# Two thirds and half of the scan steps fed row-wise instead of three fifths and seven fifteenths, in a Mamba, attention and expert block on one Trainium2 core

## The reference, cut to what matters

```
x (8, 256, 256), ctx (8, 256, 256); 2 Mamba layers, d_inner 512, d_state 64
for each layer:                                # x = x + mamba(mamba(x)), then layernorm
    u, z = split(x @ in_w.T);  u = silu(causal_conv4(u))
    dt, B, C = split(u @ xp_w.T);  dt = softplus(dt @ dtw.T + dtb)
    for t in 256:  h = h * exp(dt_t * A) + (dt_t * u_t) * B_t        # h: 512 x 64
                   y_t = (h * C_t).sum(state)
    out = ((y + u * D) * silu(z)) @ out_w.T
x = layernorm(x + attention(q from x, k and v from ctx))
x = layernorm(x + top-2-of-8 experts(x), hidden 1024)
```

## Time and profile before

| | |
|---|---|
| median of 3 runs | 3373.1 us (3371.58 to 3378.8) |
| the profiled execution's own time | 3370.43 us |
| its span | 3368.7 us |
| VectorE busy | 3042.1 us, 90% of the span |
| ScalarE busy | 2746.9 us, 82% |
| TensorE matmuls | 2734.9 us, 81% |
| GpSimd busy | 2671.6 us, 79% |
| granted TensorE clock, mean | 0.946 |

### The profile page before, as it was taken

The page is one execution under the profiler, slowest core; times in us unless marked ns, Lnnn a source line. Parts: engine busy times, 40 slices in busy tenths (PEclk is TensorE's granted clock), DMA queues, the critical chain, the costliest instruction groups (busy, mean ns, idle before and its releaser), DMA issues.

```text
span 3368.7 us, 54626 instructions
## 1 busy us (share of the span) xinstructions
PE 2734.9 (81%) x19466; PEld 2403.0 (71%) x19466; DVE 3042.1 (90%) x2196; ACT 2746.9 (82%) x6432; POOL 2671.6 (79%) x1299
## 2 busy tenths in 40 slices
PE   5878788888778877888888888878888777888876
PEld 4767677777767766777776777767777666777665
DVE  4999999999999999999999999999999999999500
ACT  6979898898978897897989888898898869888422
POOL 5989998898989788787888888787887878877401
PEclk7999999999999999999999999999999979999988
DMA  2242111111111113223231333313222122433485
GB/s 94 90 140 70 45 51 49 51 55 45 49 58 53 39 51 104 95 82 114 95 119 64 110 117 120 126 67 127 100 102 93 49 82 86 146 124 128 133 283 186
DMA packets 151747, 319.34 MB, mean 95 GB/s; under 512 B 28570, under 2 KB 44963, under 8 KB 151092
## 3 DMA queue, kind: packets, MB, share of 16 engines
q1 hardware_dynamic: 147522, 305.08, 27.1%
q0 software_dynamic: 3072, 8.39, 0.7%
q10 hardware_dynamic: 882, 2.38, 0.2%
HBM read 285.90 MB, written 29.88 MB: 94 GB/s over the span
## 4 chain that ended last, share of the span: by engine, by line
DVE 27%; issue 26%; ACT 17%; PE 15%; POOL 14%; DMA 1%; SPq 0%; POOLq 0%; DVEq 0%; ACTq 0%
DVE h L1128 14%; POOL hC L904 12%; DVE psX L1118 9%; ACT dA L1096 8%; PE psY L1395 4%; PE psG L1342 4%; ACT xs L1067 3%; PE psX L1379 2%; PE psX L1377 1%; PE psG L1421 1%; PE psX L1342 1%; PE psX L1421 1%; ACT gT L953 1%; ACT diag_b L1065 1%; DVE gT L1142 1%
## 5 line engine op out<-in xcount | busy, mean ns | idle before, releaser
L904 POOL TENSOR_TENSOR hC<-h,cb 128x1024 f32<-128x1024 f32 x1024 | 2406.0, 2371 | 464.2 <-DVE h L1128 457.2
L1128 DVE TENSOR_TENSOR_SCAN h<-dA,psX 128x1024 f32<-128x1024 f32 (+1 forms) x1115 | 2305.6, 2101 | 69.7 <-PE psX L1379 33.8
L1096 ACT ACTIVATE dA<-dt,negA 128x255 f32<-128x255 f32 x4096 | 1716.6, 503 | 103.2 <-DVE h L1128 99.9
L1395 PE MATMUL psY<-ident,hC 128*128 128x128 f32 x8192 | 1121.4, 282 | 48.6 <-DVE gT L1142 38.4
L1395 PEld LDWEIGHTS psY<-ident,hC 128*128 128x128 f32 x8192 | 976.0, 146 | 62.6 <-DVE gT L1142 42.0
L1118 DVE TENSOR_TENSOR psX<-dtu,psX 128x1024 f32<-128x1024 f32 x513 | 619.3, 1207 | 47.1 <-POOL dtu L846 35.5
L1379 PE MATMUL psX<-ident,xs 128*128 128x128 f32 x3280 | 462.0, 287 | 158.8 <-ACT xs L1067 79.6
L1067 ACT ACTIVATE xs<-dtuT,bT 128x512 f32<-128x512 f32 x820 | 546.0, 719 | 13.6 <-PE psX L1379 13.0
L1379 PEld LDWEIGHTS psX<-ident,xs 128*128 128x128 f32 x3280 | 383.9, 147 | 235.2 <-ACT xs L1067 150.1
L1366 PE MATMUL psX<-ident,bT 128*128 128x128 f32 x1026 | 218.6, 296 | 193.4 <-DVE h L1128 191.0
L1366 PEld LDWEIGHTS psX<-ident,bT 128*128 128x128 f32 x1026 | 118.3, 142 | 299.2 <-DVE h L1128 279.3
(11 more groups left out here) (198 smaller groups left out, 2000.8 us busy)
## 6 DMA issues: line engine op xcount, KB each, us to landing
cb<-c_dram SPq DMA_DIRECT2D x256, 512.0 KB, 3.7
w_up<-in_w_exp SPq DMA_DIRECT2D x196, 256.0 KB, 3.0
w_down<-in_w_exp SPq DMA_DIRECT2D x196, 256.0 KB, 3.0
dA<-in_w_exp SPq DMA_DIRECT2D x44, 256.0 KB, 4.3
h<-in_w_exp SPq DMA_DIRECT2D x44, 256.0 KB, 4.8
x_slots<-got SPq DMA_DIRECT2D x16, 512.0 KB, 5.4
xg<-x_slots SPq DMA_DIRECT2D x60, 128.0 KB, 2.8
y_slots<-yg SPq DMA_DIRECT2D x60, 128.0 KB, 3.1
```

The costliest lines, as they stand in the source:

```text
L904: eng.tensor_tensor(hC[i % NHC][:, :, :], h[i % NH][:, :, :], cw.to_broadcast([P, KI, L]), ALU.mult).then_inc(times_c, 1)
L1096: made = eng.activation(dA[j % NA][:, c, 1:L], dt[n % 2][:, c, 1:L], ACT.Exp, scale=negA[:, JOBS[n][0], c, s:s + 1])
L1128: made = eng.tensor_tensor_scan(h[i % NH][:, part, :].rearrange("p c t -> p (c t)"), dA[i % NA][:, part, :].rearrange("p c t -> p (c t)"), ...
L1395: made = eng.matmul(psY[:, tc, c * P:(c + 1) * P], hC[i % NHC][:, c, tc * P:(tc + 1) * P], ident[:, :], start=s == 0 and c == 0, stop=s == ...
```

## The change

Of the steps of jobs 0 to 5, 20 in 30 are row-wise instead of 18; of those of jobs 6 to 13, 15 in 30 instead of 14; jobs 14 and 15 stay at 14. In jobs 0 to 5 every row-wise step that follows a plain one is of form D (before, a third of them was X). `xs` becomes two tiles used in turn (NX), so that `scale_row` waits for the X step before the last. The press on rank 0 starts at s = 30 with 150 ns a step instead of at s = 44 with 300. `xrow` of the next row is loaded at the piece `norm2` of this row instead of at the next row's `turn`, and the plan places `proj` of a row only after `norm2` of the row before. The counts that follow from `is_turned` and `is_scaled_later`:

| | row-wise | D | X | plain |
|---|---|---|---|---|
| jobs 0 to 5, before | 221 | 101 | 120 | 163 |
| jobs 0 to 5, after | 244 | 122 | 122 | 140 |
| jobs 6 to 13, before | 232 | 0 | 232 | 280 |
| jobs 6 to 13, after | 256 | 0 | 256 | 256 |
| jobs 14 and 15, both | 58 | 0 | 58 | 70 |

After the change the steps run `. D X` over and over in jobs 0 to 5, and `. X` in jobs 6 to 13.

```diff
-SHARE = [18] * 6 + [14] * (NJ - 6)
+SHARE = [20] * 6 + [15] * (NJ - 8) + [14] * 2
...
-    return 12 < i < STEPS and (s + 1) * SHARE[job] // 30 > s * SHARE[job] // 30
+    return 12 < i < STEPS and s >= 0 and (s + 1) * SHARE[job] // 30 > s * SHARE[job] // 30
...
-    return is_turned(i) and not is_turned(i - 1) and i < 6 * S and i % 3 != 0
+    return is_turned(i) and not is_turned(i - 1) and i < 6 * S
...
-LIKE_IT = {i: max((t for t in TURNED if t < i and is_scaled_later(t) == is_scaled_later(i)), default=None) for i in TURNED}
+LIKE_IT = {i: [t for t in TURNED if t < i and is_scaled_later(t) == is_scaled_later(i)] for i in TURNED}
+TILES_OF = {False: NX, True: 1}
+SAME_TILE = {i: before[-TILES_OF[is_scaled_later(i)]] if len(before) >= TILES_OF[is_scaled_later(i)] else None for i, before in LIKE_IT.items()}
...
-PRESS_FROM, PRESS = 44, 300
+PRESS_FROM, PRESS = 30, 150
...
-        out += [task("proj", b, 0, "PE", 2 * MM, *copied, opens="G"),
+        out += [task("proj", b, 0, "PE", 2 * MM, *copied, *((("norm2", b - 1, 0),) if b else ()), opens="G"),
...
-                    at["ACT"] = scaled[i] = max(at["ACT"], fill_end.get(LIKE_IT[i], never)) + (600 if is_scaled_later(i) else SCALE)
+                    at["ACT"] = scaled[i] = max(at["ACT"], fill_end.get(SAME_TILE[i], never)) + (600 if is_scaled_later(i) else SCALE)
...
-        xs = sb("xs", [P, KL, DI])
+        xs = [sb(f"xs{i}", [P, KL, DI]) for i in range(NX)]
...
-                        on.wait_ge(normed[1], b)
-                        eng.dma_start(xrow[:, :, :], io["x"][b]).then_inc(xrow_in, 16)
+                            eng.dma_start(xrow[:, :, :], io["x"][0]).then_inc(xrow_in, 16)
+                    elif name == "norm2" and n + 1 < ROWS:
+                        on.wait_ge(normed[1], n + 1)
+                        eng.dma_start(xrow[:, :, :], io["x"][n + 1]).then_inc(xrow_in, 16)
...
-                if LIKE_IT[i] is not None:
-                    on.wait_ge(x_in, LIKE_IT[i] + 1)
+                at = len(LIKE_IT[i]) % NX
+                if SAME_TILE[i] is not None:
+                    on.wait_ge(x_in, SAME_TILE[i] + 1)
```

More of the change, by code:

```diff
@@ L37 @@
 NW = 3
+NX = 2
 NT = 9
@@ L1066, in scale_row @@
                     else:
-                        made = eng.activation(xs[:, tc, :], dtuT[n % 2][:, tc, :], ACT.Identity, scale=bT[n % 2][:, tc, s:s + 1])
+                        made = eng.activation(xs[at][:, tc, :], dtuT[n % 2][:, tc, :], ACT.Identity, scale=bT[n % 2][:, tc, s:s + 1])
                 made.then_inc(scaled, 1)
@@ L1378, in turn_x @@
                         else:
-                            made = eng.transpose(to, xs[:, tc, c * P:(c + 1) * P], ident[:, :])
+                            made = eng.transpose(to, xs[len(LIKE_IT[i]) % NX][:, tc, c * P:(c + 1) * P], ident[:, :])
                 made.then_inc(x_in, 1)
```

## The result

| | before | after |
|---|---|---|
| median of 19 runs | 3376.1 us | 3384.9 us |
| ratio | | 1.0022, 95% interval 1.0012 to 1.0032 |
| profiled execution | 3370.4 us | 3388.5 us |
| granted TensorE clock, mean | 0.946 | 0.948 |

A forecast was written before the change was run, and what follows sets the result against it. The prediction took VectorE to set the loop's pace. Its terms, -59.2 + 8 + 5 + 12 - 2 = -36.2 us, gave a span of 3332.5 us and a forecast median of 3337 us, range 3312 to 3366.

The forecast's parts named there:

- The first term: In jobs 0 to 13, 47 plain steps become row-wise, each saving VectorE 1.26 us: 59.2 us less.
- More waits on VectorE: In the loop, X fills made late by ScalarE's in-order queue: +8 us in jobs 0 to 5, +5 in jobs 6 to 13.
- The order of the small work: After the loop, 3 to 4 more expert tiles left over by the plan, room for 2 during routing: +12 us.
- The third, that the tiles pile up: After the loop, 13 more tiles left, 11 of them bare: +88 us instead of +12, 3413 us; chance 0.10.
- The second: Jobs 0 to 5: ScalarE takes over as pacing engine, 17 us plus some 6 us more waits, 3360 us; chance 0.15.
- the case with a chance of 0.08: After the loop, a backlog of 5 to 8 tiles eats the gain to about nothing; chance 0.08.
- The first, the full gain: Whole kernel: no term beside the 59.2 us costs anything, giving 3314 us; chance 0.17.
- over 250 us after the loop: Sign that the forecast is wrong: the part after the loop, expected at about 230 us, lasts over 250.
- ScalarE in jobs 1 to 5: Sign that the forecast is wrong: ScalarE is busy over 95% in jobs 1 to 5.
- The second `xs` tile: On ScalarE, freeing its waits for a fill to release xs: worth 0 to 13 us, taken as 0.
- `xrow` at -2 us: After the loop, row 7's early load lets its first use start sooner: 0 to 5.2 us, taken as -2.
- Waits in jobs 6 to 13 at +5: VectorE's idle time in jobs 6 to 13 grows as ScalarE fills: bounds 0 and +15 us, taken as +5.

The follow-up runs named there:

- e4: e3 with 15 in 30 steps row-wise in jobs 6 to 13 and the plan's ScalarE costs at 1650 ns (dA) and 1300 ns (X); ratio 0.9887 to before.
- e5: e4 with the share of jobs 6 to 13 back at 14 in 30; ratio 0.9979 to the kernel before.
- e7: e1 with the silu replaced by a copy, so without both table loads a job (output not the reference's); ratio 0.9885 to the kernel before.
- e8: The kernel before with the silu replaced by a copy, without both table loads a job (output not the reference's); ratio 0.9940 to the kernel before.
- e1: The change in jobs 0 to 5 alone, with jobs 6 to 15 kept at 14 in 30 row-wise steps; ratio 0.9967 to the kernel before.
- e12: e7 with only the first of the two ScalarE instructions of each log kept (output not the reference's); ratio 0.9860 to the kernel before.
- e9: e1 with six extra identity transposes on TensorE ahead of each of the 122 D fills; ratio 0.9968 to the kernel before.
- e2: The change with one xs tile instead of two; ratio 1.0014 to the kernel before.
- e6: e1 with the old rule for D steps, a third of the row-wise steps after a plain one being X again; ratio 1.0069 to the kernel before.
- e10: The whole change with the plan's cost of dA on ScalarE at 1670 ns instead of 1700; ratio 0.9977 to the kernel before.
- e3: The kernel before with only the early xrow load, the new need of proj and the second xs tile; ratio 1.0007 to the kernel before.

## Why the prediction was wrong

**The first term was right.** 47 plain steps less are worth 1.26 us each in VectorE's work, and in jobs 6 to 13, where row-wise steps have no row-wise neighbour, in time: e4 against e5 gives 34.6 us for 24 of them.

**The step that failed first: "More waits on VectorE", +8 us for jobs 0 to 5.** It measured 26.8 us in the profiled pair and 24 over all profiles. I took the waits behind X fills alone and scaled them with the number of neighbouring row-wise pairs or left them as they were; the bounds, 0 and 12 us, were both too low. In jobs 1 to 5 these waits did not grow (16.4 and 16.9 us). Those behind D fills, for dA and for the spread B, which the term left out, rose from 13.1 to 38.4. What the runs show is a third thing. A piece of the next job sits ahead of a fill or of a dA in an in-order queue; how late the scan comes depends on how much VectorE work lies between. In `. D X` three scans have one product among them, and the lead that ScalarE and TensorE have is used up by one silu piece (3.42 us late and 1.06 us more). e7 and e8 show it with the same cut, 20.1 against 8.4 us. It explains 12 of the 26 us between e1 and the kernel before. For the rest, e12 shows that pieces take turns: with the silu and half the log gone, a piece of `dtu` stands in the way twice, for 3.6 us of the waits that came anew. That all of what is left is of this kind is argued from such waits and not shown. Against the other candidates there are numbers: the clock (e9, 4 us), the `xs` tile (e2), and, unless they cancel, D fills and ScalarE's sum (e6).

The windows misled me here. I read the sum of ScalarE's and GpSimd's work against the stage (91%) and concluded that it fits; ScalarE is busy 811 of 926 us in jobs 1 to 5 after the change, less than feared, and the loss came all the same.

**The step that failed second: "The order of the small work", +12 us.** It measured 37 us, and jobs 14 and 15 another 24, for which the sum had no term. The forecast of 3 to 4 more tiles is not far from the five. Wrong were two things. No more than about one tile hides in TensorE's gap while row 7 is routed: with 18, 19, 21, 22 and 23 left the part lasts 223.7 to 225.4, 221.0 to 224.2, 246.3, 243.7 and 257.7 to 260.8 us, (260.8 - 223.7) / 5 = 7.4 us a tile from 18 on. And the routing of the rows was counted as fixed, while the three lists slipped by 57, 69 and 97 us (45, 11 and 24 in e1, so part of it starts in jobs 0 to 5). The 30th tile slipped by 246 us, more than the 100 us of slack ahead of the third list; e10 shows that a backlog comes of such tiles even with the list on time. That the plan's room on ScalarE holds rows and tiles back is what its rules say, and e10 gives back 17 of the 37 us for 30 ns a step; how the slip passes from row to row was not followed. Row 5 is now routed, and the third list written, in jobs 14 and 15: 13 us more busy time of VectorE there, and 10 us of waits.

**Rivals.** The third, that the tiles pile up, had the mechanism and the place, with 37 us instead of the 88 at its bound. The second had the place of the other loss, jobs 0 to 5, but not its cause: ScalarE's sum is not full there (968 of 1108 us), and e6 adds 31 us to it, with TensorE relieved, without harm. Nearest was the case with a chance of 0.08, five to eight tiles that eat the gain to about nothing. The five tiles came, but by the forecast's own price they cost (5 - 2) x 8.0 = 24 us, too few to eat a gain of 59, so that case would have been met in part by luck. Both losses came at once, which no case of the forecast held: 27 us of idle time, 37 after the loop and 24 in jobs 14 and 15 outweigh the 59 us of the products and the 12 us more that jobs 6 to 13 gained. That is the profiled pair; by the medians the balance is 9 us milder. The first, the full gain, is out. Of the prediction's two signs of being wrong one came, over 250 us after the loop (260.8); ScalarE in jobs 1 to 5 stayed at 88%.

**Small terms.** The second `xs` tile at 0: right. `xrow` at -2 us: 0, since the load was never late; the first use still comes 14 us after the loop's end. Waits in jobs 6 to 13 at +5: they fell by 2.6. The D fill at 2.10 us: 260.1 / 122 = 2.13 us, so the row and not the factor of four holds again.

**What stays open.** How much of the lost room is due to the new need of `proj`, the new press or the new D rule was not separated; e3 shows that `proj` costs nothing at the old shares, and e6 against e1 only that the new D rule leaves two tiles fewer than the old one would at these shares. A version with the later share alone at the plan's old costs was not run, nor one with both shares and e4's costs.

## What to carry to other kernels

When an engine that sets the pace is relieved, ask two questions of the others: whether their sum fits, and how late the longest single piece in each in-order queue makes the next critical instruction once less of the pacing work lies in between. The second question accounts for at least 12 of the 26 us lost in jobs 0 to 5. And where a plan with fixed costs orders the work, a change of the main loop is also a change of the plan: work that no longer fits by the plan's clock runs later where nothing hides it, at full price. Calibrate the plan's costs to the trace before a share is judged: 30 ns in 1700 moved the whole change from +0.22% to -0.23% (e10), and with 50 ns in 1700 and 40 in 1340 off the costs the later share alone was worth 0.9% (e4 against e5).

## What the runs showed of the hardware

The granted clock of TensorE rose and held with transposes alone: in the kernel before, from 1285.3 to 1324.4 us in job 6, TensorE ran 172 transposes and no other multiply. The clock was high (1.00) until 1299.1, low (0.50) until 1302.5, high again until 1319.5, then low until 1323.0. Over jobs 6 to 13, where the fills and the sums are all transposes and multiplies of the experts and projections run among them, its mean is 0.95 to 0.96. A D fill, eight fp32 products of 128x128x128 that the trace records as sixteen multiplies, took 2.10 to 2.13 us on average against 1.11 to 1.13 us for an X fill of eight transposes. Nine of e1's 122 D fills took 3.36 to 3.78 us, at a mean granted clock of 0.50 to 0.56. Six extra transposes ahead of each of 122 D fills, 57 us more of TensorE's busy time in jobs 0 to 5 (924 to 981), cost VectorE nothing (63.3 us of waits against 67.1).
